# A transformer-and-S4D layer on one core: taps spread by TensorE instead of a transfer, and the order of work on GpSimd and VectorE rearranged

## What is computed

```
x = x + attention(layernorm(x))      # a second layernorm with gamma, beta; q, k, v; causal softmax;
                                     # out @ o_proj, plus its own input as residual
x = x + ffn(layernorm(x))            # w rounded to float8_e4m3fn
x = x + s4d(layernorm(x))            # convolution over an axis of length 2 (the batch)
x = x + ffn(layernorm(x))            # the same weights again

def ffn(x):   return ((silu((x @ q8(gate_w)) * gate_scale)) * ((x @ q8(up_w)) * up_scale)) @ q8(down_w) * down_scale
def s4d(x):   # k = 2 Re(sum_n C (exp(dtA) - 1) / A * exp(dtA l)), l = 0, 1
              # out[0] = k[0] x[0] + D x[0];  out[1] = k[0] x[1] + k[1] x[0] + D x[1]
```

## Time and profile before

| what | us |
|---|---|
| median of 3 runs | 141.14 (140.97 to 142.03) |
| the profiled execution | 140.71 |
| its span, first to last instruction | 138.9 |
| start of FFN pass 0 on PE | 58.67 |
| start of FFN pass 1 on PE | 77.24 |
| busy in the span: PE, DVE, POOL, ACT | 117.4, 104.2, 90.1, 71.2 |

### The profile page before, as it was taken

The page is one execution under the profiler, slowest core; times in us unless marked ns, Lnnn a source line. Parts: engine busy times, 40 slices in busy tenths (PEclk is TensorE's granted clock), DMA queues, the critical chain, the costliest instruction groups (busy, mean ns, idle before and its releaser), DMA issues.

```text
span 138.9 us, 2048 instructions
## 1 busy us (share of the span) xinstructions
PE 117.4 (85%) x658; PEld 76.4 (55%) x658; DVE 104.2 (75%) x234; ACT 71.2 (51%) x131; POOL 90.1 (65%) x162
## 2 busy tenths in 40 slices
PE   5995959999929997999679997976998946999950
PEld 5782628577618856844349544556444536446630
DVE  0599999364997498679525999999999998567272
ACT  3233367797443365867475262983373453474500
POOL 2274899999995558078853547699689842029621
PEclk9999999999995999999999999999999999999998
DMA  4999800000000000000000310000000000001204
GB/s 119 280 280 373 281 1 7 0 0 0 0 0 2 2 5 0 0 0 0 1 0 5 45 30 0 2 0 5 0 0 0 0 2 0 5 0 52 99 0 151
DMA packets 6355, 6.07 MB, mean 44 GB/s; under 512 B 1685, under 2 KB 5705, under 8 KB 6345
## 3 DMA queue, kind: packets, MB, share of 16 engines
q1 hardware_dynamic: 5464, 5.91, 14.0%
q10 hardware_dynamic: 816, 0.02, 0.3%
q0 software_dynamic: 64, 0.02, 0.1%
HBM read 4.89 MB, written 1.05 MB: 43 GB/s over the span
## 4 chain that ended last, share of the span: by engine, by line
DVE 37%; PE 33%; POOL 12%; issue 9%; ACT 4%; DMA 2%; POOLq 0%; DVEq 0%; ACTq 0%
PE psum L1157 9%; PE psum L1170 7%; DVE stats L655 6%; PE psum L1036 5%; DVE fused L924 4%; PE psum L1071 4%; POOL rstd L290 4%; DVE scaled_down L872 3%; PE psum L1096 3%; PE psum L1029 3%; DVE normed L895 2%; DVE h_rows L913 2%; DVE down_raw L750 2%; DMA x_in<-in_x 2%; POOL down L434 2%
## 5 line engine op out<-in xcount | busy, mean ns | idle before, releaser
L610 ACT ACTIVATE gated<-psum,scales 128x512 f32<-128x512 f32 x24 | 16.4, 681 | 14.6 <-PE psum L1157 14.5
L1170 PE MATMUL psum<-down,f_head 128*128 128x256 bf16 x96 | 22.0, 273 | 2.0 <-POOL f_tail L443 1.9
L924 DVE SCALAR_TENSOR_TENSOR fused<-psum,up_scales_fit,gated 128x512 f32<-128x512 f32 x24 | 17.7, 739 | 7.1 <-PE psum L1157 4.5
L443 POOL TENSOR_TENSOR f_tail<-fused,f_head 128x512 f16<-128x512 f32 x12 | 14.0, 1171 | 13.4 <-ACT f_head L621 13.3
L1170 PE MATMUL psum<-down,f_tail 128*128 128x256 bf16 x96 | 22.0, 273 | 0.0
L621 ACT ACTIVATE f_head<-fused 128x512 f16<-128x512 f32 x24 | 15.0, 625 | 11.2 <-DVE fused L924 11.1
L1157 PE MATMUL psum<-h_head,up 128*128 128x512 f16 x48 | 14.3, 379 | 1.1 <-DVE fused L924 1.1
L1157 PE MATMUL psum<-h_tail,gate 128*128 128x512 f16 x48 | 14.3, 379 | 0.0
L1157 PE MATMUL psum<-h_tail,up 128*128 128x512 f16 x48 | 14.3, 379 | 0.0
L1157 PE MATMUL psum<-h_head,gate 128*128 128x512 f16 x48 | 14.3, 379 | 0.0
L931 DVE TENSOR_TENSOR f_tail<-fused,f_head 128x512 f16<-128x512 f32 x12 | 9.4, 779 | 5.7 <-ACT f_head L621 5.7
(11 more groups left out here) (166 smaller groups left out, 260.9 us busy)
## 6 DMA issues: line engine op xcount, KB each, us to landing
x_in<-in_x SPq DMA_DIRECT2D x4, 256.0 KB, 4.6
out<-x_in SPq DMA_DIRECT2D x4, 256.0 KB, 2.1
qkv_sb<-in_qkv SPq DMA_DIRECT2D x3, 256.0 KB, 4.3
gate_raw<-in_gate_w SPq DMA_DIRECT2D x1, 768.0 KB, 6.4
up_raw<-in_up_w SPq DMA_DIRECT2D x1, 768.0 KB, 8.3
down_raw<-in_down_w SPq DMA_DIRECT2D x1, 768.0 KB, 10.0
wo_sb<-in_o_proj SPq DMA_DIRECT2D x1, 256.0 KB, 5.7
taps_all<-taps_dram SPq DMA_DIRECT2D x1, 256.0 KB, 3.5
```

The lines of the kernel that those rows point to most:

```text
L443: pool.tensor_tensor(f_tail[:, m, :], fused[:, m % FUSED, :], f_head[:, m, :], ALU.subtract).then_inc(f_tail_by_pool, 1)
L610: act.activation(gated[:, m % 2, :], psum[:, BANK_GATE[m % 2], :], ACT.Silu, scale=gate_scales[:, m:m + 1]).then_inc(gated_ready, 1)
L924: dve.scalar_tensor_tensor(out=fused[:, m % FUSED, :], in0=psum[:, BANK_UP[m % 2], :], scalar=up_scales_fit[:, m:m + 1], in1=gated[:, m % ...
L1170: last = pe.matmul(column(BANK_DOWN[t // 2], H * (t % 2), H), part[:, m, t * P:t * P + P], down16[:, m, :], start=(m == 0 and t % 2 == 0 a ...
```

## The change

It does six things.

1. SP's three transfers of the taps go. PE multiplies each column of `taps`, broadcast to 128 x 128, with the identity (`spread_taps`, four products, after `gate_up(0, 1)`), and ACT copies the 512 results from PSUM to `taps_all`. `down(0, 0)`, which writes to the same bank, waits for that copy.
2. On POOL, `taps_begin` goes ahead of `inverse_std(1, 0, 2)`, `taps_middle` and the power for `bound` ahead of `inverse_std(1, 2, 2)`, and `taps_end` ahead of the six `down16` instructions.
3. On DVE, `exp_times_dt` goes behind `xn_chunk(0)` and the statistics of tiles 4 to 7.
4. `lift_down` goes ahead of `row_max(0)`, `v_half(0)` behind it, `lower_down` behind that and ahead of `g_chunk(1)`; `largest_weight(0)` goes ahead of `magnitude`.
5. `fit_powers` goes ahead of `attention_out(5)`.
6. `largest_weight(1)` moves into FFN pass 0 behind `fuse(0, 1)`, and `largest_weight(2)` behind `fuse(0, 3)`.

```diff
@@ SP @@
-            sp.wait_ge(taps_ready, 1)
-            with nc.allow_non_contiguous_dma(reason="256 taps, one per partition"):
-                for k in range(2):
-                    sp.dma_start(taps_dram.ap()[k].rearrange("(c p) -> p c", p=P), taps[:, k, :]).then_inc(taps_stored, 16)
-            sp.wait_ge(taps_stored, 32)
-            sp.dma_start(taps_all[:], taps_dram.ap().partition_broadcast(P)).then_inc(taps_loaded, 16)
@@ POOL @@
             round_weight(1, up16, gate_up_ready)
+            taps_begin()
             inverse_std(1, 0, 2, negative_mean=True)
-            taps_begin()
-            inverse_std(1, 2, 2, negative_mean=True)
+            taps_middle()
             pool.wait_ge(bound_squared, 1)
             pool.tensor_tensor(bound[:, 4, :], bound[:, 3, :], pos_half[:], ALU.pow).then_inc(bound_ready, 1)
-            taps_middle()
+            inverse_std(1, 2, 2, negative_mean=True)
+            taps_end()
             pool.wait_ge(fit_ready, 1)
             pool.wait_ge(down_rounded, 1)
...
             inverse_std(1, T, 2, negative_mean=True)
-            taps_end()
             inverse_std(1, T + 2, 2, negative_mean=True)
@@ ACT, FFN pass @@
+                    if n == 0 and m == 0:
+                        act.wait_ge(taps_spread, 1)
+                        act.activation(taps_all[:].rearrange("p k h -> p (k h)"), psum[:, BANK_DOWN[1], :],
+                                       ACT.Copy).then_inc(taps_loaded, 1)
@@ DVE @@
             exp_finish()
-            exp_times_dt()
             xn_chunk(0)
             first_stats(T)
             first_stats(T + 2)
+            exp_times_dt()
             reduce_angle()
             weight_grid(0)
             g_chunk(0)
             weight_grid(1)
             xn_chunk(1)
             weight_grid(2)
+            lift_down()
+            row_max(0)
             v_half(0)
-            row_max(0)
+            lower_down()
             g_chunk(1)
             row_max(1)
-            lift_down()
+            dve.wait_ge(gate_up_ready, 1)
+            largest_weight(0)
             magnitude()
             v_half(1)
             for k in range(2, K):
                 row_max(k)
-                if k == 2:
-                    lower_down()
-                if k == 3:
-                    dve.wait_ge(gate_up_ready, 1)
-                    largest_weight(0)
-                if k == 6:
-                    dve.wait_ge(gate_up_ready, 2)
-                    largest_weight(1)
                 if k == 5:
                     read_norms()
                     bound_gate_up()
+                if k == K - 1:
+                    fit_powers()
                 attention_out(k - 2)
             attention_out(K - 2)
             h_tails(0)
-            fit_powers()
             attention_out(K - 1)
@@ DVE, FFN pass 0 @@
                         if n == 0 and m == 1:
+                            dve.wait_ge(gate_up_ready, 2)
+                            largest_weight(1)
+                        if n == 0 and m == 3:
                             dve.wait_ge(down_rounded, 1)
                             largest_weight(2)
@@ PE @@
                 pe.wait_ge(down_ready, m + 1)
+                if n == 0 and m == 0:
+                    pe.wait_ge(taps_loaded, 1)
...
+            def spread_taps():
+
+                pe.wait_ge(taps_ready, 1)
+                pe.wait_ge(x1_ready, K)
+                for k in range(2):
+                    for c in range(C):
+                        last = pe.matmul(column(BANK_DOWN[1], k * H + c * P, P), taps[:, k, c:c + 1].to_broadcast([P, P]),
+                                         ident[:], start=True, stop=True)
+                last.then_inc(taps_spread, 1)
...
                     gate_up(n, m)
+                    if n == 0 and m == 1:
+                        spread_taps()
```

More of the change, by code:

```diff
@@ L141, in hybrid_layer @@
         psum = ctx.enter_context(nc.psum_tensor("psum", [P, 8, 512], F32))
-        taps_dram = nc.dram_tensor("taps_dram", (2, H), F32)
         x_loaded = [sem(f"x_loaded{n}") for n in range(K // 2)]
@@ L151, in hybrid_layer @@
         down_scale_loaded = sem("down_scale_loaded")
-        taps_stored, taps_loaded, out_stored = sem("taps_stored"), sem("taps_loaded"), sem("out_stored")
+        taps_spread, taps_loaded, out_stored = sem("taps_spread"), sem("taps_loaded"), sem("out_stored")
         pool_step = sem("pool_step")
@@ L451, in lag_tap @@
             def lag_tap():
-                pool.wait_ge(taps_loaded, 16)
+                pool.wait_ge(taps_loaded, 1)
                 for t in range(T):
@@ L891, in s4d_begin @@
             def s4d_begin(tiles):
-                dve.wait_ge(taps_loaded, 16)
+                dve.wait_ge(taps_loaded, 1)
                 for k in tiles:
```

## The result

Four timed executions of the changed kernel lie at 134.78 to 135.09, median 134.83; beside them the kernel before had 141.58 (140.97 to 142.20). The ratio is 0.953, 95% interval 0.947 to 0.958. Repeated in a later set beside eleven executions of before (median 140.81), it was 0.965 (0.958 to 0.972). The forecast was 136.1 in 134.6 to 138.2: the direction and the range held, the gain was larger than forecast.

A forecast was written before the change was run, and what follows sets the result against it. Side work between attention steps and PE's waits were taken to bound the kernel. 140.71 less 3.5 (start of pass 0) less 1.5 (pass 0) gives 135.7; the median lies 0.43 above, 136.1, range 134.6 to 138.2.

The forecast's parts named there:

- What binds, and where: Up to pass 0: side work between attention steps (3.28, 1.72); in PE's order, waits of 2.67 and 1.92.
- The side of PE, DVE and ACT: Before pass 0: row_max(3) 2.5 earlier, clock staying high 1.5, so normalising possible 4.0 earlier, at 50.9.
- The side of POOL: Before pass 0: rounding ends at 41.4, then 10.3 of work; POOL sets normalising at 51.7, 3.2 earlier.
- Pass 0: FFN pass 0: PE's wait of 1.92 for POOL's first tail goes whole, late searches are covered; 1.5 shorter.
- The products: FFN pass 0: the four float32 products of spread_taps cost 0.43, or 1.1 if their tails are not overlapped.
- The transfer: The old transfers of the taps landed at 81.0, ahead of the first reader at 83.4; removing them gives nothing.
- Behind pass 1: Passes 1 to 3 take as long as before within 0.5.
- Lifts late: Rival before pass 0: each lift and lower on DVE takes 2.02, total 137.2; chance 0.12.
- the wait before `turn_probs(0)`: Sign before pass 0: PE waiting there for over 1.5 (lifts too slow) would make the prediction wrong.
- rule of the exclusive lock: DVE beside POOL's rounding: a lift or lower could wait for a whole rounding instruction, 2.2; Lifts late becomes 137.9.
- The clock's fall in the attention stage: Rival: PE idles about 1.8 before turning h, the clock falls over attend(7) and pass 0, +1.5, 137.6; chance 0.16.
- POOL's small instructions: Rival before pass 0: they stretch beside DVE at 0.6 each, 144.5 with half of 29 stretched; chance 0.05.

The follow-up runs named there:

- c1: The changed kernel with lower_down put back behind row_max(2): 138.74 to 139.43 in five executions with one clock fall, 140.22 with two.
- b2: The kernel before with parts 2 and 5 alone (POOL's order, fit_powers ahead of attention_out(5)): median 139.97, ratio 0.986.
- b4: The kernel before with twelve turns of the identity on PE in the wait ahead of attend(2): median 140.97, ratio 0.993.
- c4: The kernel before with turns of the identity filling four PE waits (make_g(0), turn_z(1), attend(2), turn_h(3, 1)): 139.02 to 139.37, ratio 0.986.
- a4: The changed kernel with POOL's taps_middle behind the power for bound and inverse_std(1, 2, 2): 134.53 to 134.70 without a clock fall, median 135.41.
- b3: The kernel before with parts 3, 4 and 6 alone (exp_times_dt, lift and lower, the three searches): median 137.44, ratio 0.967.
- a3: The changed kernel with the four spreading products written as turns (pe.transpose): 134.19 to 134.32 without a clock fall, median 134.92.
- a2: The changed kernel with the taps sent by transfer again, without products and copy: 133.71 and 133.72 without a clock fall, median 135.18.
- b1: The kernel before with part 1 alone (taps spread by PE and copied by ACT): median 146.51, ratio 1.035.
- a1: The changed kernel run again without any edit: 134.76 to 134.87 without a clock fall, median 135.51.
- c2: The changed kernel with the edits of a2 and a4 together: 133.62 and 133.72 without a clock fall, 135.16 to 135.76 with one.

## Why the prediction held, point by point

**What binds, and where.** Right. The search for what stands between two steps of attention, and the replay of each engine's order, gave the start of pass 0 within 0.6 and the start of pass 1 within 0.4. c1 shows the first claim by itself, b2 the second: the wait in pass 0 belonged to POOL's queue behind `fit_powers`.

**The side of PE, DVE and ACT.** Forecast: normalising possible at 50.9. The trace: ACT was free at 50.84. `row_max(3)` stood at 37.66 against 39.59, 1.9 earlier and not 2.5, since the scores came 0.55 later (37.40 against 36.85) behind PE's wait for `v_half(0)`; the clock gave 1.4 (b4, c4) where I took 1.5. ACT was free 4.1 earlier, so 0.8 remains. I had left `largest_weight(1)`, "up to 1.7 more", out of the 4.0, and it had stood between `attend(2)` and the normalisation; no run moves it by itself, so that it gave the 0.8 is argued and not shown. That the 50.9 came out is luck: the errors cancel.

**The side of POOL.** Forecast 51.7, measured 51.14, and this is the 0.6 by which the start of pass 0 was missed. The mis-sized term is the end of rounding: 41.4 forecast (41.1 to 41.9), 40.63 measured. Its parts were right: a start at 17.1 (17.28), the gate weight stretched (10.9 by five stretched instructions of six, 11.0 measured), the up weight unstretched (7.5). But added as the prediction states them, 41.97 - 1.5, + 0.7 to 1.4, - 1.3 to 1.4, they make 39.8 to 40.6. I wrote down 41.1 to 41.9, 1.3 more at either end, for which I named no row. POOL was last by 0.3 (a4: worth 0.2) instead of 0.8. "POOL sets the start of pass 0" was true by 0.3, and its new order has no share in the gain there: b3 has the early start without it.

**Pass 0.** The wait went whole, as said, and both late searches were covered: PE is gapless to 71.96. The products cost 0.89 where I took 0.43. The failed step is the choice of the nearest row: I took the turning of h, "the same shape and the same identity", and kept 1.1 for a reason (tails not overlapped) that has nothing to do with it. The row of `scores(0)` in the profile of before would have told: two float32 products of 128 x 128 are four instructions and take 0.44 until the next one.

```profile
24.30 0.61 PE L1071 MATMUL psum<-xn_cols,g_cols 128*128 128x128 f32 x4
24.74 0.22 PE L1073 MATMUL psum<-mask,ident 128*128 128x128 bf16 x1
```

a3 shows it by turning the one into the other.

**The transfer.** Hidden, as said; a2 confirms it and prices the replacement at 1.0.

**Behind pass 1.** I said "as long as before within 0.5"; they were 0.65 shorter. PE's wait before `turn_h(2, 1)` is 1.33 instead of 1.67, and the wait of 0.41 ahead of an up product in pass 2 is gone. Both come with DVE's parts: b3's trace has 1.33 and no wait of 0.41, b2's has 1.68 and 0.41. Which of the parts 3, 4 and 6 does it no run shows.

**The rivals.** Lifts late: in part, they took 3.85 for the pair, as by the worst rows, but the lowers took 0.95 each; the wait before `turn_probs(0)` came to 1.7, past the 1.5 that I had set as a sign, but cost only the 0.55 named above. The Trainium skill's rule of the exclusive lock (SBUF — State Buffer, Who interferes with whom) allowed up to 2.2 for a lift beside rounding; the trace agrees, with 3.85 for two, 1.9 each. The clock's fall in the attention stage came in neither profile of the changed kernel: PE's wait for the rows of h, which I put at 1.8, doesn't exist, as ACT and POOL were in time. The reason that I gave for weighing it, that a wait of 1.92 is followed by no fall, doesn't hold beyond that profile: in b3 the clock fell to 0.50 at 67, behind the 1.94. POOL's small instructions ran at 0.2.

**The size.** In the profiled pair 5.93 was gained against 5.0 forecast: 4.08 for the start (3.5), 1.20 for pass 0 (1.5), 0.65 behind. 1.4 of the 4.08 is the fall at 42, which the profile of before happened to have. Of the 6.75 between the first medians not all is the order of work. Without falls it is 139.3 (c4) to 139.7 against 134.8, 4.5 to 4.9 us or 3.4%; the rest is that the kernel before had one or two falls in 33 of the 35 executions whose clock is listed, and the changed one had none in seven of ten. By equal falls the parts are b3's 3.2 and b2's 2.2, less 0.9 for the products. What I read in the profile of before as a property of one wait was one draw, and the forecast of 5.0 counted it as a gain of the change.

## What to carry to other kernels

Side work on an engine is judged by the two steps between which it stands, not by its length: two DVE instructions were worth 2.5 us by their place alone. A transfer that lands long before its reader is free, and what replaces it on the engine that bounds the stage is not. To price an added instruction take a row of the same operation, not only of the same shape.

## What the hardware showed unexpectedly

A float32 product of 128 x 128 is two instructions on PE and takes 0.22; a turn of the same size is one and takes 0.11 (four of them: 0.89 in the profile after, 0.44 in a3).

The fall of PE's clock is not tied to one place. By the mean clocks one kernel has none, one or two in different executions. In the traces it came at 21 (b1, b2), behind waits of 1.05 and 0.53; at 42 (before), behind 2.67; at 66 and 67 (b1, b3), in the stall of 4.59 and behind 1.94; and between 109 and 116 (a2, a4, b2, c1, b4), in or behind the 2.69 before `turn_h(3, 1)`. That same wait (2.69 or 2.70) stands in the traces of before, after, a1, a3, b1, b3 and c2 without a fall. A fall costs 1.2 to 1.6 (1.4 by the traces of before and c4, the rest by the steps of a1, a2 and b3). Turns of the identity in four such waits took the falls away in all six executions of c4 and with them 1.7 of the median (139.3 against 141.0), with no change of order; in one wait alone (b4) they left eight of ten with a fall. It follows that one profile says little about which wait makes the clock fall, and that kernels closer than 1% are to be compared at an equal number of falls, or by the same stretch in two traces, counted from an instruction that both have: the start of `make_g(0)` lay anywhere from 11.6 to 12.3 in the nine traces of kernels that are the same up to there.
